# Last mixture's outputs added into the result by accumulating scatters, and the value products of the attention stream in one lot a step later

## The reference

```python
x = x + tanh(g_xattn[l]) * attention_l(layernorm(x), ctx, ctx)   # 16 heads of 8, 64 keys
x = x + tanh(g_ffn[l]) * ffn_l(layernorm(x))
# ffn_0: 8 experts, top 2, and a shared expert   ffn_1: one ternary 128x128 matrix
# ffn_2: experts with fixed gates, 4 computed    ffn_3 (the last mixture), t = tokens:
route_prob = softmax(t @ switch_w + switch_b)
route_prob_max, routes = max(route_prob), argmax(route_prob)
out = (gelu(t @ w1[routes] + b1[routes]) @ w2[routes] + b2[routes]) * route_prob_max
```

## Time and profile before

| | us |
|---|---|
| median of 3 runs (1065.4 to 1068.12) | 1066.78 |
| profiled execution, span | 1063.2 |
| PE busy in it | 920.2 (87%) |
| DVE, ACT, POOL busy | 730.1, 640.2, 631.6 |
| stream (first scores to last projection) | about 421 to 938 |
| last mixture (first to last product) | 947 to 1047 |
| stretch after the last product | 16 |

### The profile page before, as it was taken

How to read it: one execution, slowest core, us unless ns; L and a number is a source line. 1 busy time by engine, 2 the same in 40 slices (tenths; PEclk the granted TensorE clock), 3 DMA queues, 4 the chain that set the end, 5 groups by cost and what they waited for, 6 DMA issues and landing times.

```text
span 1063.2 us, 23492 instructions
## 1 busy us (share of the span) xinstructions
PE 920.2 (87%) x8395; PEld 748.4 (70%) x8395; DVE 730.1 (69%) x1618; ACT 640.2 (60%) x1496; POOL 631.6 (59%) x706
## 2 busy tenths in 40 slices
PE   2788888898898998778799899999999988768993
PEld 1566666676898987456676776777777776658993
DVE  6899998363477686578788885555555568836674
ACT  2666776433665666688677776555555566444662
POOL 0467676547772472888777574444444466636753
PEclk9899999999899999899899999999999999868997
DMA  8970000001432341000000000000500000022334
GB/s 237 329 231 2 1 2 2 1 28 52 120 91 60 92 116 41 24 26 24 10 3 1 2 2 2 2 1 2 164 17 2 1 2 2 27 56 62 94 95 146
DMA packets 76852, 57.64 MB, mean 54 GB/s; under 512 B 13603, under 2 KB 69539, under 8 KB 76548
## 3 DMA queue, kind: packets, MB, share of 16 engines
q1 hardware_dynamic: 70148, 42.59, 14.2%
q0 software_dynamic: 6592, 13.58, 4.2%
HBM read 35.30 MB, written 24.08 MB: 56 GB/s over the span
## 4 chain that ended last, share of the span: by engine, by line
PE 56%; POOL 14%; DVE 11%; issue 9%; ACT 6%; DMA 2%; SPq 1%; DVEq 0%; POOLq 0%; ACTq 0%
PE psS L1209 9%; PE psT L1763 6%; PE psO L1827 5%; PE psS L1819 5%; PE psO L1219 5%; PE psS L1219 4%; PE psO L1778 4%; PE psS L1752 3%; POOL sorted_x L1439 3%; POOL ring L847 3%; PE psO L1785 2%; PE psO L1718 2%; PE psM L1739 2%; POOL sorted_z L1452 1%; POOL lnr L890 1%
## 5 line engine op out<-in xcount | busy, mean ns | idle before, releaser
L2152 POOL TENSOR_TENSOR ring<-ring,mx 128x1024 f32<-128x1024 f32 x94 | 178.2, 1903 | 119.4 <-DVE mx L2029 118.7
L1912 ACT ACTIVATE pT<-psT 128x512 f32<-128x512 f32 x192 | 114.3, 595 | 134.1 <-PE psT L1763 134.0
L1266 ACT ACTIVATE pT<-psS,b1copy 128x128 f32<-128x128 f32 x468 | 133.4, 368 | 82.9 <-PE psS L1209 82.9
L1763 PE MATMUL psT<-ident,ring 128*128 128x128 f32 x768 | 125.3, 287 | 26.5 <-POOL ring L2152 14.5
L1209 PE MATMUL psS<-ring 128*128 128x128 f32 x936 | 129.9, 284 | 13.9 <-DVE ring L1324 7.8
L1763 PEld LDWEIGHTS psT<-ident,ring 128*128 128x128 f32 x768 | 88.2, 145 | 67.5 <-issue 35.6
L1209 PEld LDWEIGHTS psS<-ring 128*128 128x128 f32 x936 | 118.7, 199 | 17.1 <-issue 8.2
L2021 DVE TENSOR_TENSOR ring<-psS,bias 128x1024 f32<-128x1024 f32 x96 | 112.9, 1218 | 22.0 <-PE psS L1752 21.4
L2029 DVE TENSOR_REDUCE mx<-ring 128x16 f32<-128x1024 f32 x96 | 112.2, 1209 | 0.0
L1321 DVE COPY ring<-w 128x512 f32 x117 | 54.4, 465 | 56.0 <-PE psO L1219 30.2
L1414 POOL DMA_INDIRECT xrows<-sorted_y,rows x64 | 61.8, 966 | 50.9 <-DMA sorted_y<-pT 33.0
(11 more groups left out here) (304 smaller groups left out, 2105.3 us busy)
## 6 DMA issues: line engine op xcount, KB each, us to landing
w<-w_dram SPq DMA_DIRECT2D x34, 256.0 KB, 6.0
sorted_x<-late SPq DMA_DIRECT2D x18, 256.0 KB, 3.4
ring<-sorted_x SPq DMA_DIRECT2D x18, 256.0 KB, 2.9
sorted_y<-pT SPq DMA_DIRECT2D x17, 256.0 KB, 2.6
sorted_z<-blank_dram SPq DMA_DIRECT2D x2, 1584.0 KB, 9.8
ring<-sorted_z SPq DMA_DIRECT2D x12, 256.0 KB
xrows<-token_y SPq DMA_DIRECT2D x8, 256.0 KB, 3.5
ctxz<-ctxz_dram SPq DMA_DIRECT2D x1, 1056.0 KB, 5.9
```

Source lines behind the costliest of these rows:

```text
L1266: op = nc.scalar.activation(hs[:, j % 2, f, :], psS[:, j % 2, f * P:(f + 1) * P], func, bias=b1copy[:, j % 4, f:f + 1])
L1763: mm = nc.tensor.transpose(psT[:, i * P:(i + 1) * P], ring[:, u % NS, p * P:(p + 1) * P], ident[:])
L1912: nc.scalar.activation(pT[:, u % 2, 4 * h:4 * h + 4, :].rearrange("p a q -> p (a q)"), psT[:, :], ACT.Exp).then_inc(s_pT, 1)
L2152: nc.gpsimd.tensor_tensor(rows_, rows_, mx[:, u % 4, 0:NH].rearrange("p h -> p h ()").broadcast_to([P, NH, SK]), ALU.subtract).then_inc(s_ ...
```

## The change

One part concerns the end, the other the stream.

*Accumulating scatters.* The result tensor gets extra rows for the padding. SP stores x itself to `out`, by halves, when the last attention has been added (`residuals_of`); POOL's 46 scatters then add to `out` (`compute_op=ALU.add`) and replace the reload, the combination and the final store. So the gate must be multiplied before the scatter. It is computed ahead of the ranks (`gates`, now with tanh(x/2) in place of the exponential, so that ACT keeps its function table), travels with the row in column 129 of `sorted_z`, comes back with the token number (`tokens_of`, two numbers a row) and multiplies each output tile (second instruction in `outputs` and `output_of_one`).

*The stream.* `weigh_values` takes a whole batch: eight products of 256 columns, at the start of the next step, ahead of the turns. Around it PE's and ACT's lists are rebuilt: the norm rows move ahead of the second turn, `turn_outputs` ahead of `turn_heads`, `keep_heads` one exponential later, the last exponential of a step ahead of half the keys, `scale_fetched` and `normalise`.

```diff
-        ids = sb("ids", [P, 2, LAST_HALF], I32)
+        ids = sb("ids", [P, 2, LAST_HALF, 2], I32)
+        pwz = ids[:].rearrange("p h t o -> p (h t o)").bitcast(F32).rearrange("p (h t o) -> p h t o", h=2, o=2)[:, :, :, 1]
...
             def tokens_of(h):
-                sp_.dma_start(ids[:, h, :], sorted_z[h][0:LAST_HALF * P, D:D + 1].bitcast(I32).rearrange("(t p) o -> p (t o)", p=P), allow_slow_non_contiguous=True).then_inc(s_ids[h], 16)
-            def outputs_of(h):
...
+                sp_.dma_start(ids[:, h, :, :], sorted_z[h][0:LAST_HALF * P, D:D + 2].bitcast(I32).rearrange("(t p) o -> p t o", p=P), allow_slow_non_contiguous=True).then_inc(s_ids[h], 16)
+
+            def residuals_of(h):
+                sp_.wait_ge(s_res, NB - (1 - h) * (B // 2))
+                sp_.dma_start(out[h * HT * P:(h + 1) * HT * P].rearrange("(t p) d -> p t d", p=P), x[:, h * HT:(h + 1) * HT, :]).then_inc(s_out[h], 16)
+
+            residuals_of(0)
             for h in range(2):
                 sp_.wait_ge(s_sc[1][h], HT * 16)
                 load(h * n)
                 load(h * n + 1)
                 tokens_of(h)
+                if h == 0:
+                    residuals_of(1)
                 for g in range(2, n):
                     load(h * n + g)
-                    if h and g == 3:
-                        outputs_of(0)
-            outputs_of(1)
+            for k in range(YS):
+                sp_.wait_ge(s_ys[k], scattered(k, 2 * n))
...
-            for c0, c1 in ((0, NC // 2), (NC // 2, NC // 2 + 2), (NC // 2 + 2, NC - 1), (NC - 1, NC)):
-                sp_.wait_ge(*FF[3].x(c1))
-                sp_.dma_start(out[c0 * CT:c1 * CT].rearrange("(t p) d -> p t d", p=P), x[:, c0 * CH:c1 * CH, :]).then_inc(s_out, 16)
-            sp_.wait_ge(s_out, 4 * 16)
+            for h in range(2):
+                sp_.wait_ge(s_out[h], 16)
...
+                step(nc.vector.tensor_tensor(pr, pr, over(m), ALU.subtract))
+                assert done[0] == LOWERED
+
+            def gates():
+
+                dve.wait_ge(s_gates[1], h + 1)
+                step(nc.vector.tensor_scalar(tmp, pr, -1.0, 1.0, ALU.mult, ALU.add))
+                step(nc.vector.reciprocal(tmp, tmp))
+                step(nc.vector.scalar_tensor_tensor(tmp, pr, 1.0, tmp, ALU.add, ALU.mult))
+                step(nc.vector.tensor_reduce(sm, tmp, AXX, ALU.add))
+                step(nc.vector.reciprocal(sm, sm))
+                dve.wait_ge(s_token, 2)
+                at = h * HT
+                for rows_, low, high in ((rows_low, 0, LOW * CH), (rows_high, LOW * CH, NT)):
+                    a, b = max(at, low), min(at + HT, high)
+                    if a < b:
+                        step(nc.vector.tensor_scalar(rows_[:, a - low:b - low, D + 1], sm[:, a - at:b - at], tg[:, LAYERS + 3:LAYERS + 4], None, ALU.mult))
+                assert done[0] == GATED[h]
 
...
-                step(nc.vector.tensor_tensor(pr, pr, over(m), ALU.subtract))
-                assert done[0] == SHIFTED
-
-            def gates():
...
 
         def gates_scalar(act, h):
-            act.wait_ge(s_half[h], SHIFTED)
-            nc.scalar.activation(rt3[h][:, 0], rt3[h][:, 0], ACT.Exp).then_inc(s_gates[1], 1)
+            act.wait_ge(s_half[h], LOWERED)
+            nc.scalar.activation(rt3[h][:, 0], rt3[h][:, 0], ACT.Tanh, scale=0.5).then_inc(s_gates[1], 1)
...
+                    if r and j == GATES_TILE:
+                        gates_scalar(act, 1)
...
-        def combine_last(dve, h, cc)
...
-                nc.vector.tensor_tensor(yslots[g % YS][:, t * P:(t + 1) * P], moe_out[1][:, (first_tile(1, g) + t) % 2, t * P:(t + 1) * P], b2copy[:, g % 2, t, :], ALU.add).then_inc(q.ye.sem, 1)
+                y = yslots[g % YS][:, t * P:(t + 1) * P]
+                nc.vector.tensor_tensor(y, moe_out[1][:, (first_tile(1, g) + t) % 2, t * P:(t + 1) * P], b2copy[:, g % 2, t, :], ALU.add).then_inc(q.ix.sem, 1)
+                dve.wait_ge(*q.ix(outputs_before(g) + t + 1))
+                k = g % (GROUPS[1] // 2) * CH + t
+                nc.vector.tensor_scalar(y, y, pwz[:, g // (GROUPS[1] // 2), k:k + 1], None, ALU.mult).then_inc(q.ye.sem, 1)
...
-                    nc.vector.tensor_tensor(yslots[g % YS][:, 0:n * P], moe_out[r][:, s, 0:n * P], b2copy[:, s, 0:n].rearrange("p t d -> p (t d)"), ALU.add).then_inc(q.ye.sem, 1)
+                    y, half, k = yslots[g % YS][:, 0:n * P], g // (GROUPS[1] // 2), g % (GROUPS[1] // 2) * CH
+                    nc.vector.tensor_tensor(y, moe_out[r][:, s, 0:n * P], b2copy[:, s, 0:n].rearrange("p t d -> p (t d)"), ALU.add).then_inc(q.ix.sem, 1)
+                    dve.wait_ge(*q.ix(g + 1))
+                    dve.wait_ge(s_ids[half], 16)
+                    rows_ = y.rearrange("p (t d) -> p t d", d=D)
+                    nc.vector.tensor_tensor(rows_, rows_, pwz[:, half, k:k + n].rearrange("p t -> p t ()").broadcast_to([P, n, D]), ALU.mult).then_inc(q.ye.sem, 1)
...
+                if r and g == 0:
+                    second_gates()
                 outputs(g)
                 if r and g == 0:
                     rank_second()
-            if r:
-                second_gates()
-                for cc in range(NC // 2):
-                    combine_last(dve, 1, cc)
...
+                    pool.wait_ge(s_out[g // n], 16)
                 for t in range(group_size(1, g)):
                     pool.wait_ge(*q.ye(outputs_before(g) + (t + 1 if g >= SINGLE else 1)))
-                    nc.gpsimd.indirect_dma_start(token_y[g // n], bass.IndirectOffsetOnAxis(ids[:, g // n, g % n * CH + t:g % n * CH + t + 1], 0),
-                                                 yslots[g % YS][:, t * P:(t + 1) * P], None).then_inc(s_ys[g % YS], 16)
+                    nc.gpsimd.indirect_dma_start(out, bass.IndirectOffsetOnAxis(ids[:, g // n, g % n * CH + t, 0:1], 0),
+                                                 yslots[g % YS][:, t * P:(t + 1) * P], None, compute_op=ALU.add).then_inc(s_ys[g % YS], 16)
...
-            def weigh_values(u):
-                n, qt = divmod(u, QT)
-                pe.wait_ge(s_pT, 2 * u + 2)
+            def weigh_values(n):
+                pe.wait_ge(s_pT, 4 * n + 4)
                 pe.wait_ge(s_free, turn["values", layer(n), n % B // 4] + 1)
-                if u == 0:
+                if n == 0:
                     pe.wait_ge(s_one, 2)
-                if qt == 0 and n:
+                else:
                     pe.wait_ge(s_on, n)
+                sums = psV.rearrange("p (t h q) -> p t h q", t=QT, h=2)
                 for half in range(2):
                     for r in range(4):
                         p = 4 * half + r
-                        at = (QT * qt + half) * P
-                        mm = nc.tensor.matmul(psV[32 * r:32 * r + 32, at:at + P], vals(layer(n), n % B, p), pT[:, qt, p, :],
+                        mm = nc.tensor.matmul(sums[32 * r:32 * r + 32, :, half, :], vals(layer(n), n % B, p), pT[:, :, p, :],
                                               start=True, stop=True, tile_position=(0, 32 * r))
                 mm.then_inc(s_pv, 1)
 
...
+                if 0 <= n - 1 < NB:
+                    weigh_values(n - 1)
                 if 0 <= n < NB:
                     turn_probs(2 * n, 0)
                 if 0 <= n + AHEAD < NB:
                     queries(n + AHEAD)
-                if 0 <= 2 * n - 1 < NU:
-                    weigh_values(2 * n - 1)
+                if query_norm(n - 1):
+                    norm_rows(("query", query_norm(n - 1)))
+                elif turn_ffn(n) is not None and not behind(turn_ffn(n)):
+                    norm_rows(("ffn", turn_ffn(n)))
                 if 0 <= n < NB:
                     turn_probs(2 * n, 1)
+                if query_norm(n - 1) and turn_ffn(n) is not None and not behind(turn_ffn(n)):
+                    norm_rows(("ffn", turn_ffn(n)))
+                if 0 <= n - 1 < NB:
+                    turn_outputs(n - 1)
                 if 0 <= n - 2 < NB:
                     turn_heads(n - 2)
-                if 0 <= n - 1 < NB:
-                    turn_outputs(n - 1)
-                if query_norm(n - 1):
-                    norm_rows(("query", query_norm(n - 1)))
-                if turn_ffn(n) is not None and not behind(turn_ffn(n)):
-                    norm_rows(("ffn", turn_ffn(n)))
                 if up_at(n) is not None:
                     four_up(up_at(n), n)
                 if 0 <= n < NB:
...
                     project(n - 2)
-                if 0 <= 2 * n < NU:
-                    weigh_values(2 * n)
...
-                if 0 <= n - 2 < NB:
-                    keep_heads(n - 2)
...
+                if n == RANK_AT:
+                    gates_scalar(act, 0)
                 if 0 <= n < NB:
                     keep_probs(2 * n + 1, 0)
+                if 0 <= n - 2 < NB:
+                    keep_heads(n - 2)
...
-                    keep_keys(*keys_at(n))
+                    keep_keys(*keys_at(n), range(GH // 2))
```

(17 more changed lines are left out.)

84 lines of the change are left out of this document (34 added, 50 removed).

## The result

The changed kernel takes 1078.49 us, median of four runs (1076.33 to 1080.87), the kernel before 1067.45 (1065.40 to 1068.44): a ratio of 1.0106, interval 1.0081 to 1.0131. It is slower by 1.1%; forecast were 1054 us and a gain.

What follows compares the result with a forecast made beforehand. POOL bounds 426 to 519.5 us; PE is full in later stretches, except routing, mixture start and end. Terms -5.9 + 2.9 - 1.3 + 3.15 - 11.3 = -12.5 us from the 1066.78 median give 1054; range 1045 to 1063.

Steps and rivals of the forecast that it cites:

- The end: After the last scatter: reload, combination and stores, 12.8 us, all go; less 0.8 and 0.7, 11.3 us saved (9.3 to 12.4).
- The second rival: Adding scatters cost POOL somewhat more: at 1.43 us each 1.7 us more, at 1.5 a time of 1058 us; chance 0.14.
- The fourth rival: POOL's queue of 42 scatters bounds the whole end; gain gone at 1.75 us a scatter, 1077 us at 2.0; chance 0.07.
- the prediction's own sign of being wrong: Wrong if the last scatter comes over 3 us later than the last output, or steps with experts exceed 13.8 us.
- The landing: Time for an adding scatter's data to land, between 2.24 us and twice that; 0.7 us more than plain was taken.
- Gates before the ranks: Routing of the first half: one subtraction and seven more DVE instructions ahead of the ranks cost 2.9 us (2.3 to 3.4).
- Start of the mixture and tile 8: PE begins the mixture 1.3 us earlier; DVE's later weight copy for tile 8 adds 3.15 us, which stays.
- The stream: Joined value products and new PE and ACT order across the attention steps: -5.9 us in all (-12 to +2).

Runs made afterwards that it cites:

- stream_alone_2: The kernel before with only the stream part of the change, old gates and ending kept, run on another chip: 1058.47 us against 1067.66, ratio 0.9903.
- rows_carry_x: Stream part on the kernel before, but rows carry 1/deviation and bias, ACT restores x, plain scatters write the result: 1056.13 us against 1067.66, ratio 0.9889.

## Why the prediction was wrong

Forecast were 1054 us and a gain of 12.5; measured were 1078.5 and a loss of 11.0.

**The step that failed** is in "The end": "The last eleven scatters run without a break ... and the whole run moves by it", with a distance of 1.28 us taken over from the plain scatter. The forecast bounded an adding scatter's landing and left its price on POOL, which no row showed, at the plain one's. The second rival (0.14) let it move up to 1.5 us from start to start, only the fourth (0.07) further. It is 1.54 us, and 1.85 from start to start, so that POOL's queue and no longer the last output sets the end: the last scatter starts 23 us behind the last output, where more than 3 was the prediction's own sign of being wrong. The fourth rival's place, queue and direction are what happened. Its break-even of 1.75 us was right in kind: at 1.855 it gives 986.5 + 42 x 1.855 + 2.9 = 1067.3, and the profile after, less the 6.8 us of its entry, ends at 1072.3. The 5 us between are the next two points. (The rival counts 42 distances where 42 scatters have 41; the queue in fact starts 0.9 us later and its 41 distances have a mean of 1.876, which makes up for it. Its 1077 us at 2.0 a scatter is near the measured time partly because of the drain that it leaves out.)

**"From there to the end of the span ... are 12.8 us ... All of it goes" was wrong too.** The stores covered POOL's drain, which ends 6.1 or 7.1 us behind POOL's last scatter in every trace. Behind the last landing 4.6 us stay. Even with plain scatters the end took 8.3 us from the last scatter's start where 3.0 were forecast; before it took 15.0, so it gives 6.7 and not 12. With plain scatters this error of 5 us is made up by what the stream and the clock gave more (below), which is why that version comes out at 1055.6, near the 1054 forecast: two errors that cancel, not a sum that was right.

**The landing** takes 3.3 us instead of 2.2 to 2.3: +1.0 to 1.1 where 0.7 was taken. That is right in size, and inside the recorded 2.4 to 4.2. (With 2.4 the saving would be 12.8 - 0.8 - 0.2 = 11.8, not the 12.3 of the text.)

**Gates before the ranks**, 2.9 us (2.3 to 3.4). DVE in order of time, after:

```profile
900.63 1.24 DVE L1084 TENSOR_SCALAR ctxz<-ctxz 128x128 f32<-128x128 f32 x1
901.91 0.95 DVE L1085 RECIPROCAL ctxz<-ctxz 128x128 f32<-128x128 f32 x1
902.90 0.29 DVE L1086 SCALAR_TENSOR_TENSOR ctxz<-ctxz 128x128 f32<-128x128 f32 x1
903.23 0.29 DVE L1087 TENSOR_REDUCE rs<-ctxz 128x16 f32<-128x128 f32 x1
903.55 0.25 DVE L1088 RECIPROCAL rs<-rs 128x16 f32<-128x16 f32 x1
```

The reciprocal over 128 takes 0.95, as taken. The first instruction lasts 1.24 instead of 0.3 (0.22 in the second half; why is not shown), so the seven take 3.8 with the two small ones behind these rows, where 2.6 were taken. Against `stream_alone_2`, which has no gates there, the first row scatter comes 3.7 us later behind the same point of the stream, 0.3 above the bound. In `rows_carry_x`, with Exp in the stream and no reciprocal over 128, this is 1.5.

**Start of the mixture and tile 8.** PE after:

```profile
947.83 2.08 PE L1218 MATMUL psS<-ring 128*128 128x128 f32 x8 [0.69 <-ACT ring L1268]
...
969.13 1.88 PE L1218 MATMUL psS<-ring 128*128 128x128 f32 x8 [4.04 <-DVE ring L1328]
970.80 1.91 PE L1228 MATMUL psS<-ring,pT 128*128 128x128 f32 x8
973.84 1.13 PE L1218 MATMUL psS<-ring 128*128 128x128 f32 x8 [1.12 <-issue]
```

The start is earlier by the 1.3 us forecast (0.69 of waiting instead of 2.00). Tile 8 begins 26.0 us behind the first tile instead of 23.6, +2.4 (3.15 taken). The prediction said that this would stay, and it did not. Before, PE stood for 3.20 us in front of tile 8 and then had a granted clock of 0.50 (the lower level, 1.2 GHz) from 970 to 976.8, and tiles 8 and 9 took 3.54 and 3.44 us. Now it stands for 4.04 us in front of tile 7 and has the lower clock from 969.4 to 972.8; tile 7 runs slow, and tiles 8 and 9 take 1.85 and 2.23. This gives back 2.9. The whole is -2.0 instead of +1.85.

One more thing moved here, which the sum has at nothing. DVE now makes the second half's gates before the first outputs, so the first output scatter starts 18.0 us behind PE's first product (965.82 - 947.83) and not 14.6. That is free while POOL waits for outputs; by POOL's list a full queue hands most of it on to the end. This is argued and not measured: no run puts the gates behind these outputs.

**The stream**, forecast at -5.9, was -8.3 up to the first row scatter (`stream_alone_2`). Its parts, in the step that answers to the earlier trace rows, PE and then ACT:

```profile
711.41 1.07 PE L1786 MATMUL psO<-pT,w 128*32 128x256 f32 x16
712.41 0.66 PE L1772 MATMUL psT<-ident,ring 128*128 128x128 f32 x4
```

```profile
701.20 0.65 PE L1793 MATMUL psO<-ident,oTs 128*128 128x128 f32 x4 [0.20 <-ACT oTs L1934]
```

```profile
699.70 0.60 ACT L1922 ACTIVATE pT<-psT 128x512 f32<-128x512 f32 x1 [0.98 <-PE psT L1772]
700.19 0.47 ACT L1928 ACTIVATE qTs<-psM,bqk 128x256 f32<-128x256 f32 x1
700.55 0.60 ACT L1934 ACTIVATE oTs<-psO 128x512 f32<-128x512 f32 x1
```

The lot takes 1.00 (1.0 taken), the copy of the sums follows the queries at t + 1.54 (t + 1.56), with t = 699.01, and PE turns them at t + 2.19 (t + 2.22). From start to start the turn in front grew by 0.33 us, of which the row shows 0.20 as idle. A step with experts takes 13.41 instead of 13.38 to 13.39: +0.02 instead of +0.1, since the borders at queries and heads gave 0.16 and not 0.08. A plain step takes 7.30 instead of 7.75 to 7.85, -0.5 instead of -0.33: the wait of 0.34 went (0.50 from start to start), and the borders gave the rest. The two steps behind the keys gave 0.8 each (0.9 taken), leaving the POOL-bound part 2.0 (1.1 taken). The Trainium skill's rule ("TensorE: Matmul & The Clock Gate", Measured speedup vs the span model), by which a pack lasts one of its products and about 4 ns for each further tile, was right that joining itself gives next to nothing: 1.01 for either form. That only 0.03 us of the gain would be left does not follow, since two lots in one place lose one border as well.

So the stream, the gates and the start came within 2.5 us of their terms, and tile 8 missed by 3.7 on the good side through the clock. The fifth term, the end, was built on the price of one instruction that no row showed.

## What to carry to other kernels

When a change swaps one kind of instruction on a serial engine for another, the first unknown to bound from both sides is that instruction's own time there, times its count, and not what it does in memory; a queue with 0.15 us of slack a scatter (1.43 against 1.28) leaves no room for a guess. Before counting a tail as gain, look for what it covers: the end of the span may be held by a drain that is hidden today. And an order on PE that fills a wait with work already in the list (the turn of the norm rows, 0.9 us a step between its two places) can be worth more than any joining.

## What the runs showed of the hardware

- An indirect scatter of 128 rows of 512 bytes holds POOL for 0.96 us plain and 1.54 adding; with 64 rows 0.90 and 1.40. 0.3 us of issue stand between two. Landing 2.3 and 3.3 us. The page counts 6592 packets in POOL's queue before and 11744 after, for the same 13.58 MB: 112 more for each of the 46 scatters.
- POOL's drain at the end of the program ends 6.1 us behind its last indirect DMA in the five traces whose 46 scatters all add 128 rows, and 7.1 in the other eleven.
- DVE's reciprocal: 0.95 us over 128 numbers a partition, 0.55 over 64, 0.25 over 16.
- The same program takes 1067 us on one kind of chip and 1201 on another. The adding scatter (1.54 us) and the stream's steps (7.30, 13.41) last the same on both; the waits differ. The same change was 1.1% slower on the one kind and 1.8% faster on the other.
